# VectorE's instructions of a selective scan interleaved: scans, taps and step sizes between each other, and the next quad's first scan ahead of the high product

## The chip, the cores and the metric

The kernel runs on one core of one Trainium2 chip. The metric is device microseconds from launch to end. Five engines run side by side, each in its own order: TensorE (PE), VectorE (DVE), ScalarE (ACT), GpSimd (POOL) and SyncE (SP, here only a DMA queue). They meet through semaphores alone, also within one engine: an instruction of VectorE that reads what an earlier one of VectorE wrote waits for that one's semaphore.

## The reference, cut

All is float32; two rows of 1024 tokens, 512 wide. The part that takes the time is a state-space layer (1024 inner channels, 16 states each) with a mixture of experts beside it:

```
x, gate = split(xn @ W_in.T);  x = silu(conv4(x))
ts, B, C = rms(split(x @ W_x.T))
dt = softplus(ts @ W_dt.T + b_dt);  A = -exp(A_log)
for t:  state = state * exp(dt_t * A) + (dt_t * x_t) * B_t
        y_t   = sum_n state[n] * C_t[n]
y = (y + x * D) * silu(gate);  s = y @ W_out.T
out = hidden + s * silu(top2_experts(xn))
```

## The kernel before

The 2048 tokens are four chunks of 512 (two chunks a row of the batch); the 1024 channels are eight tiles of 128. Chunk by chunk and tile by tile gives 32 **tiles** n = 0 to 31; chunk c = n // 8, t = n % 8. In chunks 1 and 3 ("odd") the scans start from the state kept by the chunk before. The 16 states of a tile are four **quads** m = 4n to 4n + 3. A quad is four scans r = 0 to 3 of 128 x 512, each holding 32 channels times 4 states on the partitions.

What happens to a quad m:

- POOL writes its drives `drive[m % 4]` (L588, one multiplication of 128 x 2048), and runs up to four quads ahead.
- ACT writes the decays exp(dt * A) into the four PSUM banks `sc` (L801, four instructions). `decays(m, 0)` writes banks 0 and 1, `decays(m, 1)` banks 2 and 3. Since there is only one set of banks, `decays(m + 1, 0)` waits until quad m has left banks 0 and 1, and `decays(m + 1, 1)` until quad m's **high product** has read banks 2 and 3. In even chunks ACT first keeps the two last states (L780).
- DVE runs the four scans (L1175), and multiplies by C (L1185): the **high product** of r = 2, 3 always, the **low product** of r = 0, 1 only in quads that `POOL_QUADS` doesn't give to POOL (then POOL does it, L601, and the two scans write to SBUF, so that their banks come free at once). 94 of 128 low products are POOL's.
- PE sums over the states into `y_ps` (L1426).

Per tile there is more, on every engine in an order written out by hand:

- **Step sizes.** Two tiles ahead PE writes `dt_ps` (L1363), ACT does the softplus (|x|, exp, 1 + e, log: L746 to L758), and DVE ends it in three instructions, each on the one before (L1154, L1156, L1158), and `times_x` (L1150), which multiplies by x. In the tiles that `VECTOR_LOG` leaves out PE adds the parts instead, and DVE has `times_x` alone. ACT copies dt, and a DMA sends both out and back, spread over the partitions, as `rep`.
- **Convolution** of the next chunk, one or two channel tiles per tile for t = 2 to 6 of chunks 0 to 2 (`LATE_X`, `EARLY_X`). ACT copies the projection and applies the first tap (L707, L710); DVE applies the other three (L1114), each on the one before. The late one of a tile is ACT's `copy_x` between `decays(4n + 2, 1)` and `decays(4n + 3, 0)`; on DVE its three taps stand ahead of quad 4n + 3.
- **Gate.** ACT switches its table (1.28 us), does the silu of the gate and of x, and switches back, between `decays(4n + 2, 0)` and `decays(4n + 2, 1)`. DVE's `gate_tile(n - 1)` (L1202) multiplies the summed y by it, after the high product of the first quad of tile n; PE's next sums into `y_ps` wait for that.
- PE also does the gate projection, the experts' slots, the projections of the next chunk and, in the first tiles of a chunk, the output projection of the chunk before.

ACT's order in a tile is: decays(4n, 1), copy dt, decays(4n + 1, 0), copy_x early, decays(4n + 1, 1), decays(4n + 2, 0), tables and silu, decays(4n + 2, 1), copy_x late, decays(4n + 3, 0), decays(4n + 3, 1), softplus(n + 2), decays(4n + 4, 0), with small copies for the experts between. The change leaves it, and the orders of PE, POOL and the DMA queues, alone.

## Time and profile before

| | us |
| --- | --- |
| median of 3 runs | 1072.48 (1071.75 to 1073.99) |
| the profiled execution | 1074.76 |
| its span, first to last instruction | 1072.9 |
| DVE busy | 996.6 (93%) |
| POOL busy | 909.7 (85%) |
| PE busy | 861.6 (80%) |
| ACT busy | 727.6 (68%) |

The profile is one execution. Each view names an instruction by its line, engine, operation and tiles; two of a kind in a row are one line of the timeline ("x2"), with the start of the first and the time to the end of the last. A bracket is idle time of the engine just ahead, and what ended it.

### The profile page before, as it was taken

Reading aid. Unit: us, or ns where it says so; the run is one execution under the profiler, and the core shown is the slowest. Engines: PE = TensorE matmul, PEld = TensorE weight load, DVE = VectorE, ACT = ScalarE, POOL = GpSimd, SP = SyncE. Lnnn points to the kernel's source line nnn. Section 1 sums busy time; section 2 is a strip of 40 time slices with the busy share of each in tenths; the row PEclk is TensorE's granted clock in tenths of the full one; section 3 lists DMA queues with packets and bytes.
Section 4 is the critical chain, followed back from the end, with each engine's and each line's share of the span. In section 5 each row is a group of like instructions: output and inputs, shape, how many; then the busy total and the mean of one; then the engine's idle time right before and its main releaser. Section 6 shows DMA issues by size and latency. Waiting matters only on the chain.

```text
span 1072.9 us, 10234 instructions
## 1 busy us (share of the span) xinstructions
PE 861.6 (80%) x2756; PEld 319.1 (30%) x2756; DVE 996.6 (93%) x1025; ACT 727.6 (68%) x1281; POOL 909.7 (85%) x322
## 2 busy tenths in 40 slices
PE   8943557988978998898846859889897999679568
PEld 5321112333323333333211313333332343223122
DVE  6779988999999989999999899999999989999997
ACT  3657656788787766788565566688777666567543
POOL 0617898997989998888798979799988988999996
PEclk9976668999999999999876879999998999889779
DMA  9847668767778576666743752965648556664725
GB/s 336 345 158 285 223 235 330 278 247 267 263 266 333 183 270 241 228 257 212 259 113 143 217 194 109 320 231 191 228 149 303 217 215 235 216 220 182 274 42 154
DMA packets 86585, 245.93 MB, mean 229 GB/s; under 512 B 9344, under 2 KB 10752, under 8 KB 79872
## 3 DMA queue, kind: packets, MB, share of 16 engines
q1 hardware_dynamic: 67712, 197.03, 51.4%
q10 hardware_dynamic: 12672, 31.46, 7.4%
q0 software_dynamic: 6144, 16.78, 5.8%
q8 instruction: 23, 0.38, 0.1%
q14 instruction: 34, 0.28, 0.1%
HBM read 183.11 MB, written 62.13 MB: 229 GB/s over the span
## 4 chain that ended last, share of the span: by engine, by line
DVE 30%; PE 22%; POOL 21%; issue 11%; DMA 9%; ACT 5%; SPq 2%; DVEq 0%; ACTq 0%; POOLq 0%
DVE sc_ps L1175 13%; POOL drive L588 12%; DVE drive L1175 8%; PE x_ps L1458 5%; POOL drive L601 4%; PE f_ps L1411 4%; DMA rep<-rep_rows 4%; PE y_ps L1426 3%; PE dt_ps L1386 2%; DMA rep_rows<-dtu 2%; DVE x_ps L1114 2%; DVE drive L1185 2%; PE x_ps L1322 2%; POOL moe L573 2%; ACT sc_ps L801 1%
## 5 line engine op out<-in xcount | busy, mean ns | idle before, releaser
L588 POOL TENSOR_TENSOR drive<-rep,b_all 128x2048 f32<-128x2048 f32 x127 | 578.9, 4598 | 46.6 <-DMA rep<-rep_rows 40.5
L801 ACT ACTIVATE sc_ps<-rep,a_neg 128x512 f32<-128x512 f32 x512 | 332.0, 681 | 93.3 <-DVE drive L1185 63.4
L601 POOL TENSOR_TENSOR drive<-drive,c_all 128x1024 f32<-128x1024 f32 x94 | 224.2, 2385 | 20.6 <-ACT state L780 12.8
L1426 PE MATMUL y_ps<-drive,stack 128*32 128x512 f32 x1024 | 153.5, 675 | 107.1 <-POOL drive L601 59.8
L1175 DVE TENSOR_TENSOR_SCAN sc_ps<-sc_ps,state,drive 128x512 f32<-128x512 f32 x164 | 201.0, 1272 | 4.7 <-ACT sc_ps L801 2.4
L1185 DVE TENSOR_TENSOR drive<-sc_ps,c_all 128x1024 f32<-128x1024 f32 x162 | 198.4, 1224 | 5.4
L1175 DVE TENSOR_TENSOR_SCAN sc_ps<-sc_ps,drive 128x512 f32<-128x512 f32 x160 | 186.5, 1211 | 14.6 <-ACT sc_ps L801 7.4
L1411 PE MATMUL f_ps<-w_ring,xT_slot 128*128 128x512 f32 x368 | 171.8, 611 | 14.9 <-ACT xT_slot L811 14.7
L1386 PE MATMUL dt_ps<-xnT,w_g 128*128 128x512 f32 x232 | 126.8, 697 | 27.5 <-ACT dtu L768 27.5
L1175 DVE TENSOR_TENSOR_SCAN drive<-sc_ps,state,drive 128x512 f32<-128x512 f32 x92 | 112.7, 1266 | 3.4 <-ACT sc_ps L801 3.4
L1175 DVE TENSOR_TENSOR_SCAN drive<-sc_ps,drive 128x512 f32<-128x512 f32 x96 | 111.7, 1205 | 0.0
L1411 PEld LDWEIGHTS f_ps<-w_ring,xT_slot 128*128 128x128 f32 x368 | 68.9, 195 | 117.4 <-issue 116.7
L1322 PE MATMUL x_ps<-xnT,w_x 128*128 128x512 f32 x192 | 90.0, 613 | 3.1 <-DMA w_x<-wx_in 3.1
L1458 PE MATMUL x_ps<-w_out,xy 128*128 128x512 f32 x176 | 83.6, 622 | 0.0
L1386 PEld LDWEIGHTS dt_ps<-xnT,w_g 128*128 128x128 f32 x232 | 49.2, 223 | 110.3 <-issue 110.3
L1426 PEld LDWEIGHTS y_ps<-drive,stack 128*32 128x32 f32 x1024 | 21.5, 113 | 199.5 <-issue 119.1
L780 ACT ACTIVATE state<-sc_ps 128x2 f32<-128x2 f32 x80 | 13.4, 168 | 64.5 <-DVE drive L1185 63.1
L1322 PEld LDWEIGHTS x_ps<-xnT,w_x 128*128 128x128 f32 x192 | 35.6, 193 | 56.9 <-issue 52.1
L1420 PE MATMUL y_ps<-xy,diag 128*128 128x512 f32 x64 | 35.5, 638 | 17.8 <-DVE xy L1202 17.8
L1458 PEld LDWEIGHTS x_ps<-w_out,xy 128*128 128x128 f32 x176 | 32.9, 196 | 51.6 <-issue 51.0
L1363 PE MATMUL dt_ps<-dt_in,w_dt 128*128 128x512 f32 x64 | 42.2, 745 | 5.4 <-DVE dt_in L1225 4.2
L811 ACT COPY xT_slot<-f_ps 128x512 f32<-128x512 f32 x46 | 26.6, 578 | 26.1 <-PE f_ps L1400 26.1
(187 smaller groups left out, 1034.0 us busy)
## 6 DMA issues: line engine op xcount, KB each, us to landing
rep<-rep_rows SPq DMA_DIRECT2D x128, 512.0 KB
w_ring<-wring SPq DMA_DIRECT2D x46, 1024.0 KB, 5.4
rep_rows<-dtu ACTq DMA_DIRECT2D x32, 512.0 KB
x_slot<-slot_x SPq DMA_DIRECT2D x46, 256.0 KB, 7.0
slot_rows<-y_slot ACTq DMA_DIRECT2D x46, 256.0 KB
w_g<-wg_in SPq DMA_DIRECT2D x32, 256.0 KB
w_x<-wx_in SPq DMA_DIRECT2D x24, 256.0 KB
slot_x<-zeros SPq DMA_DIRECT2D x1, 5888.0 KB, 20.5
```

The source lines that it names most:

```text
L588: pool.tensor_tensor(drive[:, m % RING, :, :], rep[:, n % 2, :, 1, :], b_all[:, q:q + 1, :].broadcast_to([P, NR, TC]), ALU.mult).then_inc( ...
L601: pool.tensor_tensor(drive[:, m % RING, 0:2, :], drive[:, m % RING, 0:2, :], c_all[:, q:q + 1, :].broadcast_to([P, 2, TC]), ALU.mult).then ...
L801: act.activation(sc[:, r, :], rep[:, n % 2, r, 0, :], ACT.Exp, scale=a_neg[:, lo:lo + 1]).then_inc(decay_ok, 1)
L1175: dve.tensor_tensor_scan(to, sc[:, r, :], drive[:, m % RING, r, :], state[:, lo:lo + 1] if follows else 0.0, ALU.mult, ALU.add).then_inc(s ...
L1185: dve.tensor_tensor(drive[:, m % RING, 2 * h:2 * h + 2, :], sc[:, 2 * h:2 * h + 2, :], c_all[:, q:q + 1, :].broadcast_to([P, 2, TC]), ALU. ...
L1322: last = pe.matmul(x_bank(j), w(h), xnT[:, c % 2, h, :], start=(h == 0), stop=(h == HK - 1))
L1363: pe.matmul(dt_ps[:, :], w_dt[:, t, :], dt_in[:, :], start=True, stop=True).then_inc(dt_mm, 1)
L1386: mm = pe.matmul(gate_bank(c, t)[:, :], w_g[:, h, :], xnT[:, c % 2, h, :], start=(h == 0), stop=(h == HK - 1))
L1411: last = pe.matmul(f_ps[:, :], xT_slot[:, h, :], w_ring[:, j % 2, h, :], start=(h == 0), stop=(h == HK - 1))
L1420: pe.matmul(y_ps[:, :], diag[:, :], xy[:, c % 2, t, :], start=True, stop=False).then_inc(skip_mm, 1)
L1426: last = pe.matmul(y_ps[CH * r:CH * (r + 1), :], stack[:, :], drive[:, m % RING, r, :], start=False, stop=(m % NQ == NQ - 1))
L1458: last = pe.matmul(bank, xy[:, c % 2, t, P * i:P * (i + 1)], w_out[:, t, :], start=(t == 0), stop=(t == NT - 1))
```

## The change

Only VectorE's order changes; it computes the same with as many instructions, and two semaphores more (`tap_sum`, `part_ok`) carry the waits that `link` made.

- The three taps of a convolution stand each between two scans of a quad, no longer in a row.
- The low product stands after scan 2, no longer right after scan 1.
- `scan(m + 1, 0)`, the next quad's first scan, stands ahead of `products(m, 1)` after the second and third quad of each tile. After the first it is the gate that stands ahead of the high product, except in the 13 tiles of `GATE_BEHIND`: there it is again the next quad's scan, and the gate follows the product. After the fourth quad nothing is put between, except in the 12 tiles of `STEPS_AMONG_SCANS`.
- In those 12 tiles the three instructions of the softplus stand around the last scan and the last high product, and `times_x` after the first scan of the next tile.

```diff
+STEPS_AMONG_SCANS = (1, 3, 5, 10, 15, 16, 17, 19, 21, 26, 27, 29)
+GATE_BEHIND = (3, 5, 9, 10, 15, 18, 19, 21, 25, 26, 27, 29, 30)
...
-            def convolve(j):
+            def tap(j, k):
                 c, t = divmod(j, NT)
-                dve.wait_ge(tap_ok, j + 1)
+                if k == 1:
+                    dve.wait_ge(tap_ok, j + 1)
+                else:
+                    dve.wait_ge(tap_sum, 2 * j + k - 1)
...
+            def larger_part(k):
+                dve.wait_ge(ln_ok, k + 1)
...
+            def less_rounding(k):
+                dve.wait_ge(part_ok, 2 * (k - pe_logs(k)) + 1)
...
+            def plus_log(k):
+                dve.wait_ge(part_ok, 2 * (k - pe_logs(k)) + 2)
...
                 if n:
-                    low(m)
+                    scan(m, 0)
+                    if n - 1 in STEPS_AMONG_SCANS:
+                        times_x(n + 1)
+                    scan(m, 1)
                     if pe_log(n + 1):
                         times_x(n + 1)
-                    scans(m, 1)
+                    scan(m, 2)
+                    low_product(m)
+                    scan(m, 3)
                     if chunk_end and not pe_log(n + 1):
                         step_sizes(n + 1)
+                    if n not in GATE_BEHIND:
+                        gate_tile(n - 1)
+                    else:
+                        scan(m + 1, 0)
                     products(m, 1)
-                if n:
-                    gate_tile(n - 1)
-                low(m + 1)
+                    if n in GATE_BEHIND:
+                        gate_tile(n - 1)
+
+                if n not in GATE_BEHIND:
+                    scan(m + 1, 0)
                 if early is not None:
-                    convolve(NT * (c + 1) + early)
-                scans(m + 1, 1)
+                    tap(NT * (c + 1) + early, 1)
+                scan(m + 1, 1)
+                if early is not None:
+                    tap(NT * (c + 1) + early, 2)
+                scan(m + 1, 2)
+                low_product(m + 1)
+                if early is not None:
+                    tap(NT * (c + 1) + early, 3)
+                scan(m + 1, 3)
                 if after_odd and t == 2:
                     out_tile(c - 1, 3)
+                scan(m + 2, 0)
                 products(m + 1, 1)
-                low(m + 2)
+
+                scan(m + 2, 1)
                 if after_odd and t == 1:
                     out_tile(c - 1, 0)
-                high(m + 2)
-                if late is not None:
-                    convolve(NT * (c + 1) + late)
+                scan(m + 2, 2)
+                low_product(m + 2)
+                scan(m + 2, 3)
+                scan(m + 3, 0)
                 if after_odd and t == 1:
                     out_tile(c - 1, 1)
-                low(m + 3)
-                high(m + 3)
-                if rms_tile:
+                products(m + 2, 1)
+
+                if late is not None:
+                    tap(NT * (c + 1) + late, 1)
+                scan(m + 3, 1)
+                if late is not None:
+                    tap(NT * (c + 1) + late, 2)
+                scan(m + 3, 2)
+                low_product(m + 3)
+                if late is not None:
+                    tap(NT * (c + 1) + late, 3)
+                if n in STEPS_AMONG_SCANS:
+                    larger_part(n + 2)
+                scan(m + 3, 3)
+                if n in STEPS_AMONG_SCANS:
+                    less_rounding(n + 2)
+                products(m + 3, 1)
+                if n in STEPS_AMONG_SCANS:
+                    plus_log(n + 2)
+                elif rms_tile:
```

Two places in the program's order on VectorE. The first is tile 4, from its last scans of quad 17 to quad 19 (L1175 is a scan, which the listing calls SCALAR_TENSOR_TENSOR, L1185 a high product, L1114 a tap). Before:

```order
L1175 SCALAR_TENSOR_TENSOR sc_ps<-sc_ps,drive 128x512 x2
L1185 TENSOR_TENSOR drive<-sc_ps,c_all 128x1024
L1175 SCALAR_TENSOR_TENSOR drive<-sc_ps,drive 128x512 x2
L1175 SCALAR_TENSOR_TENSOR sc_ps<-sc_ps,drive 128x512 x2
L1185 TENSOR_TENSOR drive<-sc_ps,c_all 128x1024
L1114 SCALAR_TENSOR_TENSOR x_ps<-x_pad,cw,x_ps 128x512 x2
L1114 SCALAR_TENSOR_TENSOR xy<-x_pad,cw,x_ps 128x512
L1175 SCALAR_TENSOR_TENSOR drive<-sc_ps,drive 128x512 x2
L1175 SCALAR_TENSOR_TENSOR sc_ps<-sc_ps,drive 128x512 x2
L1185 TENSOR_TENSOR drive<-sc_ps,c_all 128x1024
```

The same piece on VectorE in the change, from quad 18's first scan, which stands right behind quad 17's last (scans are L1190, high products L1200, taps L1119 there):

```order
L1190 SCALAR_TENSOR_TENSOR drive<-sc_ps,drive 128x512
L1200 TENSOR_TENSOR drive<-sc_ps,c_all 128x1024
L1190 SCALAR_TENSOR_TENSOR drive<-sc_ps,drive 128x512
L1190 SCALAR_TENSOR_TENSOR sc_ps<-sc_ps,drive 128x512 x2
L1190 SCALAR_TENSOR_TENSOR drive<-sc_ps,drive 128x512
L1200 TENSOR_TENSOR drive<-sc_ps,c_all 128x1024
L1119 SCALAR_TENSOR_TENSOR x_ps<-x_pad,cw,x_ps 128x512
L1190 SCALAR_TENSOR_TENSOR drive<-sc_ps,drive 128x512
L1119 SCALAR_TENSOR_TENSOR x_ps<-x_pad,cw,x_ps 128x512
L1190 SCALAR_TENSOR_TENSOR sc_ps<-sc_ps,drive 128x512
L1119 SCALAR_TENSOR_TENSOR xy<-x_pad,cw,x_ps 128x512
L1190 SCALAR_TENSOR_TENSOR sc_ps<-sc_ps,drive 128x512
```

The first scan of quad 18 and that of quad 19 have moved ahead of the high products of quads 17 and 18, and the first scan of quad 19 now also stands ahead of all three late taps.

The second place is the end of tile 3 and the start of tile 4 on VectorE, a tile of `STEPS_AMONG_SCANS` (L1154, L1156, L1158 and L1150 are the step sizes). Before:

```order
L1175 SCALAR_TENSOR_TENSOR sc_ps<-sc_ps,drive 128x512 x2
L1185 TENSOR_TENSOR drive<-sc_ps,c_all 128x1024
L1154 SCALAR_TENSOR_TENSOR dt_ps<-dt_ps,t_e 128x512
L1156 SCALAR_TENSOR_TENSOR dt_ps<-t_w,dt_ps 128x512
L1158 TENSOR_TENSOR dt_ps<-t_l,dt_ps 128x512
L1150 TENSOR_TENSOR dtu<-dt_ps,xy 128x512
```

In the change (L1159, L1164, L1169 and L1155):

```order
L1159 SCALAR_TENSOR_TENSOR dt_ps<-dt_ps,t_e 128x512
L1190 SCALAR_TENSOR_TENSOR sc_ps<-sc_ps,drive 128x512
L1164 SCALAR_TENSOR_TENSOR dt_ps<-t_w,dt_ps 128x512
L1200 TENSOR_TENSOR drive<-sc_ps,c_all 128x1024
L1169 TENSOR_TENSOR dt_ps<-t_l,dt_ps 128x512
L1190 SCALAR_TENSOR_TENSOR drive<-sc_ps,drive 128x512
L1155 TENSOR_TENSOR dtu<-dt_ps,xy 128x512
```

The first of the softplus's three now stands ahead of the last scan, and `times_x` behind the next tile's first.

## Rows read from the trace of the kernel before

**Rows 1.** The page's head, and its busy time of each engine.
```profile
span 1072.9 us, 10234 instructions
PE 861.6 (80%) x2756; PEld 319.1 (30%) x2756; DVE 996.6 (93%) x1025; ACT 727.6 (68%) x1281; POOL 909.7 (85%) x322
```
**Rows 2.** Busy time by stretch: length, PE, PEld, DVE, ACT, POOL, clock, DMA, GB/s.
```profile
568.00:612.70 44.70, 31.39 (x95) 10.90 (x95) 41.41 (x40) 25.19 (x45) 42.53 (x22) 0.81 0.52 155
906.60:1030.40 123.80, 92.71 (x306) 32.59 (x299) 118.11 (x107) 79.46 (x125) 121.39 (x41) 0.86 0.62 213
```
**Rows 3.** Waits of VectorE, whole span: us in total, times, longest.
```profile
DVE dt_ps L1154 <- ACT t_l L755: 10.2, 7, 3.7
DVE sc_ps L1175 <- ACT sc_ps L801: 9.8, 8, 2.7
```
**Rows 4.** Timeline of VectorE in tile 4: start, us, instruction.
```profile
217.50 2.33 DVE L1175 TENSOR_TENSOR_SCAN drive<-sc_ps,drive 128x512 f32<-128x512 f32 x2
219.75 1.52 DVE L1114 SCALAR_TENSOR_TENSOR x_ps<-x_pad,cw,x_ps 128x512 f32<-128x512 f32 x2
...
221.97 2.34 DVE L1175 TENSOR_TENSOR_SCAN sc_ps<-sc_ps,drive 128x512 f32<-128x512 f32 x2
224.35 1.22 DVE L1185 TENSOR_TENSOR drive<-sc_ps,c_all 128x1024 f32<-128x1024 f32 x1
...
231.23 1.54 DVE L1114 SCALAR_TENSOR_TENSOR x_ps<-x_pad,cw,x_ps 128x512 f32<-128x512 f32 x2
...
233.47 2.33 DVE L1175 TENSOR_TENSOR_SCAN drive<-sc_ps,drive 128x512 f32<-128x512 f32 x2
```
**Rows 5.** Timeline of ScalarE in tile 4, from quad 18's first decays.
```profile
219.87 0.20 ACT L780 ACTIVATE state<-drive 128x2 f32<-128x2 f32 x1 [0.82 <-DVE drive L1175]
...
221.42 1.28 ACT L941 ACT_TABLE_LOAD   x1
...
224.37 1.28 ACT L949 ACT_TABLE_LOAD   x1
...
229.39 1.30 ACT L801 ACTIVATE sc_ps<-rep,a_neg 128x512 f32<-128x512 f32 x2
```
**Rows 6.** Timeline of VectorE in tile 10.
```profile
390.92 1.23 DVE L1185 TENSOR_TENSOR drive<-sc_ps,c_all 128x1024 f32<-128x1024 f32 x1
393.13 0.69 DVE L1202 TENSOR_TENSOR xy<-y_ps,gate 128x512 f32<-128x512 f32 x1 [0.99 <-PE y_ps L1426]
394.77 2.46 DVE L1175 TENSOR_TENSOR_SCAN drive<-sc_ps,state,drive 128x512 f32<-128x512 f32 x2 [0.94 <-ACT sc_ps L801]
...
407.73 1.55 DVE L1114 SCALAR_TENSOR_TENSOR x_ps<-x_pad,cw,x_ps 128x512 f32<-128x512 f32 x2 [0.90 <-ACT x_ps L710]
```
**Rows 7.** Timeline of VectorE from tile 23 into tile 24.
```profile
817.81 1.22 DVE L1185 TENSOR_TENSOR drive<-sc_ps,c_all 128x1024 f32<-128x1024 f32 x1
...
825.31 2.46 DVE L1175 TENSOR_TENSOR_SCAN drive<-sc_ps,state,drive 128x512 f32<-128x512 f32 x2 [0.54 <-ACT sc_ps L801]
```
**Rows 8.** Timeline of ScalarE from tile 23 into tile 24.
```profile
819.27 1.30 ACT L801 ACTIVATE sc_ps<-rep,a_neg 128x512 f32<-128x512 f32 x2
821.03 0.60 ACT L746 ACTIVATE t_e<-dt_ps 128x512 f32<-128x512 f32 x1 [0.46 <-PE dt_ps L1363]
...
824.49 1.30 ACT L801 ACTIVATE sc_ps<-rep,a_neg 128x512 f32<-128x512 f32 x2
```
**Rows 9.** Timeline of tile 17, VectorE and ScalarE.
```profile
622.71 1.22 DVE L1185 TENSOR_TENSOR drive<-sc_ps,c_all 128x1024 f32<-128x1024 f32 x1
...
630.69 1.30 ACT L801 ACTIVATE sc_ps<-rep,a_neg 128x512 f32<-128x512 f32 x2
...
631.47 2.34 DVE L1175 TENSOR_TENSOR_SCAN sc_ps<-sc_ps,drive 128x512 f32<-128x512 f32 x2
```
**Rows 10.** Timeline of VectorE where it waits for POOL.
```profile
612.70 2.35 DVE L1175 TENSOR_TENSOR_SCAN sc_ps<-sc_ps,drive 128x512 f32<-128x512 f32 x2 [1.98 <-POOL drive L588]
...
1030.45 2.47 DVE L1175 TENSOR_TENSOR_SCAN sc_ps<-sc_ps,state,drive 128x512 f32<-128x512 f32 x2 [2.35 <-POOL drive L588]
```

More of the change, by code:

```diff
@@ L1103, in route_weights, with convolve @@
                 dve.tensor_tensor(p2[:, :], e2, r1, ALU.mult).then_inc(prob_ok, 1)
-            def convolve(j):
+            def tap(j, k):
                 c, t = divmod(j, NT)
-                dve.wait_ge(tap_ok, j + 1)
-                if c == 1:
+                if k == 1:
+                    dve.wait_ge(tap_ok, j + 1)
+                else:
+                    dve.wait_ge(tap_sum, 2 * j + k - 1)
+                if k == K - 1 and c == 1:
                     dve.wait_ge(s_stage, 16 * (NCH - 2))
                     dve.wait_ge(lgT_mm, 1)
-                if c >= 2:
+                if k == K - 1 and c >= 2:
                     dve.wait_ge(o_mm, TT * (c - 1))
+                dve.scalar_tensor_tensor(out=x_bank(j) if k < K - 1 else xy[:, c % 2, t, :], in0=padded(j)[:, k:k + TC],
+                                         scalar=cw[:, t * K + k:t * K + k + 1], in1=x_bank(j),
+                                         op0=ALU.mult, op1=ALU.add).then_inc(tap_sum if k < K - 1 else conv_ok, 1)
+            def convolve(j):
                 for k in range(1, K):
-                    tap = dve.scalar_tensor_tensor(out=x_bank(j) if k < K - 1 else xy[:, c % 2, t, :], in0=padded(j)[:, k:k + TC],
-                                                   scalar=cw[:, t * K + k:t * K + k + 1], in1=x_bank(j),
-                                                   op0=ALU.mult, op1=ALU.add)
-                    if k < K - 1:
-                        link(tap)
-                    else:
-                        tap.then_inc(conv_ok, 1)
+                    tap(j, k)
             spreads(1)
@@ L1169, in scans @@
                 if follows:
-                    dve.wait_ge(state_ok, kept_states(m - NQ * NT) + h + 1)
-                for r in (2 * h, 2 * h + 1):
-                    lo = column(t, q, r)
-                    to = drive[:, m % RING, r, :] if h == 0 and on_pool(m) else sc[:, r, :]
-                    dve.wait_ge(decay_ok, NR * m + r + 1)
-                    dve.tensor_tensor_scan(to, sc[:, r, :], drive[:, m % RING, r, :],
-                                           state[:, lo:lo + 1] if follows else 0.0,
-                                           ALU.mult, ALU.add).then_inc(scan_ok, 1)
+                    dve.wait_ge(state_ok, kept_states(m - NQ * NT) + r // 2 + 1)
+                lo = column(t, q, r)
+                to = drive[:, m % RING, r, :] if r < 2 and on_pool(m) else sc[:, r, :]
+                dve.wait_ge(decay_ok, NR * m + r + 1)
+                dve.tensor_tensor_scan(to, sc[:, r, :], drive[:, m % RING, r, :],
+                                       state[:, lo:lo + 1] if follows else 0.0,
+                                       ALU.mult, ALU.add).then_inc(scan_ok, 1)
             def products(m, h):
@@ L1187, in products, with low_product @@
                                   ALU.mult).then_inc(high_ok if h else low_ok, 1)
-            def low(m):
-                scans(m, 0)
+            def low_product(m):
                 if not on_pool(m):
                     products(m, 0)
-            def high(m):
-                scans(m, 1)
-                products(m, 1)
             def gate_tile(n):
@@ L1232, in _ @@
             route_rows()
-            for h in range(2):
-                scans(0, h)
-                products(0, h)
+            scan(0, 0)
+            scan(0, 1)
+            low_product(0)
+            scan(0, 2)
+            scan(0, 3)
+            products(0, 1)
             route_weights()
@@ L1245, in _ @@
                 if n:
-                    low(m)
+                    scan(m, 0)
+                    if n - 1 in STEPS_AMONG_SCANS:
+                        times_x(n + 1)
+                    scan(m, 1)
                     if pe_log(n + 1):
                         times_x(n + 1)
-                    scans(m, 1)
+                    scan(m, 2)
+                    low_product(m)
+                    scan(m, 3)
                     if chunk_end and not pe_log(n + 1):
                         step_sizes(n + 1)
+                    if n not in GATE_BEHIND:
+                        gate_tile(n - 1)
+                    else:
+                        scan(m + 1, 0)
```

21 lines of the change are left out of this document (12 added, 9 removed).

## The prediction

> **What bounds the kernel now.** Read the busy times first [rows 1]: VectorE is busy 996.6 of 1072.9 us and POOL 909.7, so VectorE is the first suspect and POOL the second. Then the busy times by stretch [rows 2] and where VectorE waits for POOL [rows 10]. In two stretches POOL hardly stops (42.53 of 44.70 us, and 121.39 of 123.80), and at the end of each VectorE stands waiting for a drive (1.98 and 2.35 us). In those 169 us it is POOL that sets the pace; work that VectorE saves there buys nothing, and up to about 2 us that it loses costs nothing. In the rest VectorE is nearly always busy. Its waits are short and mostly for ScalarE [rows 3]: 10.2 us for the logarithm and 9.8 us for decays. That looks like one engine that is the bound. The timelines of one tile [rows 4, 5] say more: VectorE and ScalarE pass the four banks back and forth, and ScalarE has stretches without idle time that end just ahead of the scan that needs them. So the question isn't only how much VectorE's work shrinks, but whether ScalarE's next decay is there earlier.
>
> **What goes.** An instruction of VectorE that doesn't wait for the one ahead starts before that one's profiled end: the scans at 217.50 end at 219.83, the first tap starts at 219.75, 0.08 us earlier [rows 4]. One that waits for the result of the one ahead starts after it: the scans at 221.97 end at 224.31, the high product starts at 224.35, 0.04 us later. The difference is 0.12 us a pair. Pairs that the change takes apart, counted in the program: 103 high products (124 stood right behind their scan; 20 at a tile's end and one before the loop stay), 33 low ones, 48 taps (24 convolutions, two each), 36 in the 12 tiles of step sizes: 220. 220 x 0.12 = 26 us of VectorE's time. No DMA and no wait on another engine is removed.
>
> The row shows 0.12 us for each wait of this kind. The Trainium skill speaks against that (VectorE: DVE Perf Modes, section "The DRAIN you can't avoid"): eight copies take as long with a semaphore after each as with one after the last, "the semaphore costs nothing extra here". By that rule the saving would be 0 and not 26 us; the trace disagrees with it, by the 0.12 us between the two kinds of pair.
>
> **What the moved steps cost.** Steps of VectorE, from start to next start [rows 4]: a scan 1.12 us (2.25 for two), a high product 1.22 - 0.08 = 1.14, a tap behind something else 0.67, three taps in a row 2.22.
>
> *Tile 4, the late convolution.* ScalarE's chain starts when quad 17's second scan ends, at 219.83, and is without idle time from 219.87: keep states, quad 18's decays, table, silu, table, decays of banks 2 and 3, a copy, copy_x (late), and quad 19's first decay at 229.39 [rows 5], done half of 1.30 us later, at 230.04: 10.2 us after the scan. Before, VectorE needed quad 19's first scan only at 233.47, 13.6 us after it: 3.4 us of cover. In the new order what stands between is two taps, two scans, quad 18's first scan, one high product and three scans: 1.33 + 2.24 + 1.12 + 1.14 + 3.36 - 0.08 = 9.1 us. The high product and the late taps, 1.14 + 2.24, have gone behind quad 19's first scan and cover nothing. VectorE waits 10.2 - 9.1 = 1.1 us. The tile saves 7 pairs, 0.84. Net +0.3 us. This is because the taps stand where ScalarE has its copy_x, and the scan has been moved past them. Worked in the same way, tiles 3, 5, 20 and 21 give 0 to +0.3 each (the first decay of their last quad also waits for PE's projection), and 11 to 13, where no states are kept, -0.1 each. Together +0.8.
>
> *Tiles 7 and 23, the softplus at the end.* With the next scan ahead of it, the third quad's high product, at 817.81, ends about one scan later (1.12 and a short wait, less two pairs: +1.0). It frees the banks for ScalarE's last decays at 819.27, and behind them in ScalarE's order stand the softplus (821.03, where it had 0.46 us to wait for PE) and the next tile's decays at 824.49, for which VectorE already waits 0.54 us at 825.31 [rows 7, 8]. So most of it is passed on: +0.8, and in tile 7 about +0.9: +1.7.
>
> *Tile 17, low products on VectorE.* ScalarE's chain starts here with the low product, which ends at 623.93; the second decay pair of quad 70 begins at 630.69 and its first is done at 631.34, 7.4 us later, and VectorE needs it at 631.47 [rows 9]. There is no cover at all. Now the low product comes a scan later (+1.12), and the next quad's low product (1.14) has moved from ahead of that scan to behind it. Against it stand 11 pairs, 1.3 us, and a wait for the first step size instruction that now comes about 2.4 us sooner. I take +1.4. Tiles 1 and 14 have the same form: +1.2 and +0.4. Tiles 16 and 30 lie in POOL's stretches. Tile 31 is the last: +0.7.
>
> *Tile 10, the gate behind.* The first high product, at 390.92, is done at 392.15, in the shadow of two waits, for the gate's sums (0.99) and for decays (0.94) [rows 6]. Moved behind the scan that ends this wait at 394.77, it and the gate cost 1.14 + 0.60 us there. 0.90 is given back at 407.73, where VectorE waits for copy_x anyway; but quad 43's first scan now stands ahead of quad 42's high product, and copy_x ahead of that scan's decay. +1.0, between 0 and +2.4. Tiles 25 and 26 have the same form; there it is PE, busy without a break, that sets when the next rep is sent, and only the later gate counts: +0.7. In tile 19 the moved scan fills a wait for the gate, but two later ones appear at quads 78 and 79, about a scan each, against its 11 pairs: I take +1.3, from below nothing to 2; its neighbour 18 +0.2.
>
> *Step sizes among the scans.* The first of them needs the logarithm, which ends 3.7 us after the high product of the third quad, since that frees ScalarE's last decays (1.30 us) and four activations follow. In tiles 26, 27 and 29 VectorE is there after two scans: 1.4 us of wait against 0.84 saved. They lie in POOL's second stretch, whose cover is 2.35 us; I count +0.5. Tiles 6 and 22 (one convolution, the rms) come to +0.35 each; 8, 15 and 24 save 0.3 each, since they have no late tap.
>
> **Sum.** 0.8 + 1.7 + 1.4 + 1.2 + 0.4 + 0.7 + 1.0 + 0.7 + 1.3 + 0.2 + 0.5 + 0.7 - 0.9 = +9.7 us. Each of these is worked on the clock of its own tile; existing waits behind them will take some, as the one at 612.70 [rows 10] for what tiles 14 and 1 lose ahead of it, and I take off 2. The profiled execution is 1074.76 us, 2.3 above the median, so 1074.76 + 7.7 = 1082.5, and against the median 1080. What measures as different from no change is about 0.2%, 2 us.
>
> **Rivals.** (1) *ScalarE gives way.* VectorE is 93% busy and ScalarE 68% [rows 1], so it may be that waits of a microsecond in a tile are caught up by the next one, where ScalarE has slack, and the 26 us arrive outside POOL's two stretches: 26 x (1 - 169/935) = 21, 935 us being the loop behind 137 us. Less the few hard waits (5) the time is 1072.5 - 16 = 1056. For it speaks that VectorE's waits are only some 20 us in all; against it the chain of rows 5, which is as long as the tile gives room for. (2) *Half of it.* The stalls come out at half of what I worked out, as when ScalarE's copies come earlier with their inputs: 26 us is saved, of which a third stays over: -8, 1064. The decider is whether quad 4n + 3's first scan waits in the late tiles; from a wait under 0.8 us on the tile gains. (3) *Even*, within 2 us of 1072.5. (4) *Worse.* The later high products delay PE's sums and with them POOL's ring, and every tile of `STEPS_AMONG_SCANS` waits 1.4 us for its logarithm: 12 x 1.4 = 17 less what is counted: 1092. (5) *No pair costs anything*, so that only the moved waits are left. VectorE comes later by the 0.12 us of each pair, which makes its waits shorter: +12, 1084. Rows 4 speak against it; the Trainium skill, in the section named above, would have it so.
>
> **Chances.** Forecast (1074.6 to 1088) 0.46; worse 0.07; no pair costs anything 0.02; even 0.13; half 0.20; ScalarE gives way 0.12. That makes slower 0.55, the same 0.13, faster 0.32. The forecast's own range is 1075 to 1088. The range reaches down to the half gain and to the upper part of ScalarE's giving way, to 1058, and up to 1091.
>
> **What the new profile would show.** Right: high products start 0.08 us ahead of the end of what stands before them, and VectorE's busy time hardly falls while its waits for ScalarE's decays grow from 9.8 to 30 us or more, most of them at the first scan of a tile's last quad (tiles 3 to 5, 10 to 13, 18 to 21); in tiles 26, 27 and 29 a wait for the logarithm; at the start of tiles 8 and 24 a wait for decays of 1 us. Wrong: tile 4 shorter than before, those waits absent. The forecast is wrong in the main if ScalarE's decays for the last quad come earlier than 10.2 us after the scan that starts their chain.

## The result, and the profile after

The change makes the kernel slower: 1085.47 us (median of 4 runs, 1083.90 to 1088.65) against 1072.12, a ratio of 1.0125 (95% interval 1.0107 to 1.0143). The predicted time was 1080.0, from 1058 to 1091.

The page of the kernel after, its head and the busy time of each engine:

```profile
span 1084.2 us, 10364 instructions
PE 859.8 (79%) x2756; PEld 319.6 (29%) x2756; DVE 976.2 (90%) x1025; ACT 728.0 (67%) x1281; POOL 910.2 (84%) x322
```

Against [rows 1] the span is 11.3 us longer, VectorE's busy time 20.4 us shorter, and the others are as they were. So VectorE has its saving, and 31.7 us more of idle time. The waits of VectorE after (us in total, times, longest) say for whom:

```profile
DVE drive L1190 <- ACT sc_ps L804: 28.6, 15, 5.1
DVE sc_ps L1190 <- ACT sc_ps L804: 20.2, 18, 2.6
DVE dt_ps L1159 <- ACT t_l L758: 15.6, 13, 3.7
DVE sc_ps L1190 <- POOL drive L591: 7.7, 4, 4.9
DVE xy L1212 <- PE y_ps L1477: 2.4, 1, 2.4
```

The two upper rows are scans that wait for decays: 48.8 us. Before, the row of [rows 3] has 9.8, and its sister (scans that write `drive`) has 3.4. Two more rows of the kernel before:

```profile
DVE xy L1202 <- PE y_ps L1426: 7.1, 5, 2.1
DVE drive L1175 <- ACT sc_ps L801: 3.4, 4, 0.9
```

So decays cost 35.6 us more, and the logarithm (15.6 against 10.2) 5.4 more. The other way went the gate's wait for PE, from 7.1 to 2.4, and the gaps inside the dependent pairs: some 0.03 us in each of the 220, 7 us.

Tile 4 after, on VectorE (start, us, instruction, and idle time in brackets):

```profile
219.35 1.21 DVE L1190 TENSOR_TENSOR_SCAN drive<-sc_ps,drive 128x512 f32<-128x512 f32 x1
...
227.39 2.32 DVE L1190 TENSOR_TENSOR_SCAN sc_ps<-sc_ps,drive 128x512 f32<-128x512 f32 x2
230.91 1.22 DVE L1190 TENSOR_TENSOR_SCAN drive<-sc_ps,drive 128x512 f32<-128x512 f32 x1 [1.20 <-ACT sc_ps L804]
232.05 1.20 DVE L1200 TENSOR_TENSOR drive<-sc_ps,c_all 128x1024 f32<-128x1024 f32 x1
233.16 0.74 DVE L1119 SCALAR_TENSOR_TENSOR x_ps<-x_pad,cw,x_ps 128x512 f32<-128x512 f32 x1
```

and on ScalarE:

```profile
220.59 0.20 ACT L783 ACTIVATE state<-drive 128x2 f32<-128x2 f32 x1 [0.77 <-DVE drive L1190]
...
229.08 0.78 ACT L713 ACTIVATE x_ps<-x_pad,cb,cw 128x512 f32<-128x512 f32 x1
...
230.11 1.30 ACT L804 ACTIVATE sc_ps<-rep,a_neg 128x512 f32<-128x512 f32 x2
```

The scan at 219.35 ends at 220.56 and starts ScalarE's chain; the first of quad 19's two decays is done at 230.11 + 0.65 = 230.76. That is 10.2 us, as forecast, and the wait is 1.20 us where 1.1 was forecast. Behind the waiting scan stand the high product and the tap that could have filled it.

### The profile page after: what moved, and what is told of

The parts are those of the page before. It is cut to its first block, busy times and chain, and to the rows that moved or that the text cites. A ratio compares the mean times of both kernels' runs of the same rounds, so it can differ in the third digit from the quotient of the medians.

```text
span 1084.2 us, 10364 instructions
## 1 busy us (share of the span) xinstructions
PE 859.8 (79%) x2756; PEld 319.6 (29%) x2756; DVE 976.2 (90%) x1025; ACT 728.0 (67%) x1281; POOL 910.2 (84%) x322
## 4 chain that ended last, share of the span: by engine, by line
DVE 24%; PE 24%; issue 15%; POOL 14%; ACT 13%; DMA 7%; SPq 2%; ACTq 1%; DVEq 0%; POOLq 0%
POOL drive L591 8%; DVE sc_ps L1190 8%; DVE drive L1200 6%; PE x_ps L1509 5%; ACT sc_ps L804 5%; PE f_ps L1462 5%; DVE drive L1190 4%; PE x_ps L1373 4%; POOL drive L604 3%; DMA rep<-rep_rows 2%; PE y_ps L1477 2%; DMA w_x<-wx_in 2%; DMA rep_rows<-dtu 2%; PE dt_ps L1437 2%; PE x_ps L1395 1%
## 5 line engine op out<-in xcount | busy, mean ns | idle before, releaser
L1190 DVE TENSOR_TENSOR_SCAN sc_ps<-sc_ps,state,drive 128x512 f32<-128x512 f32 x164 | 203.0, 1271 | 11.9 <-ACT sc_ps L804 11.3
L1190 DVE TENSOR_TENSOR_SCAN sc_ps<-sc_ps,drive 128x512 f32<-128x512 f32 x160 | 189.6, 1214 | 16.9 <-ACT sc_ps L804 8.9
L1200 DVE TENSOR_TENSOR drive<-sc_ps,c_all 128x1024 f32<-128x1024 f32 x162 | 195.3, 1206 | 0.8
L1437 PE MATMUL dt_ps<-xnT,w_g 128*128 128x512 f32 x232 | 123.7, 682 | 23.9 <-ACT dtu L771 23.7
L1190 DVE TENSOR_TENSOR_SCAN drive<-sc_ps,state,drive 128x512 f32<-128x512 f32 x92 | 115.6, 1268 | 15.9 <-ACT sc_ps L804 15.6
L1190 DVE TENSOR_TENSOR_SCAN drive<-sc_ps,drive 128x512 f32<-128x512 f32 x96 | 115.2, 1208 | 13.8 <-ACT sc_ps L804 13.0
L626 POOL TENSOR_SCALAR rep<-rep,moe 128x512 f32<-128x512 f32 x8 | 16.5, 2065 | 30.7 <-DVEq L1137 30.7
L1119 DVE SCALAR_TENSOR_TENSOR x_ps<-x_pad,cw,x_ps 128x512 f32<-128x512 f32 x54 | 39.7, 736 | 2.0 <-ACT x_ps L713 1.8
```

Source lines behind the costliest of these rows:

```text
L1119: dve.scalar_tensor_tensor(out=x_bank(j) if k < K - 1 else xy[:, c % 2, t, :], in0=padded(j)[:, k:k + TC], scalar=cw[:, t * K + k:t * K + ...
L1190: dve.tensor_tensor_scan(to, sc[:, r, :], drive[:, m % RING, r, :], state[:, lo:lo + 1] if follows else 0.0, ALU.mult, ALU.add).then_inc(s ...
L1200: dve.tensor_tensor(drive[:, m % RING, 2 * h:2 * h + 2, :], sc[:, 2 * h:2 * h + 2, :], c_all[:, q:q + 1, :].broadcast_to([P, 2, TC]), ALU. ...
L1437: mm = pe.matmul(gate_bank(c, t)[:, :], w_g[:, h, :], xnT[:, c % 2, h, :], start=(h == 0), stop=(h == HK - 1))
```

## The change, tile by tile

A tile is taken from the start of its quad 4n's second scan to that of the next tile. Its length after less its length before, in the two profiled executions, beside the prediction's terms (us):

| tiles | forecast | measured |
| --- | --- | --- |
| 3, 4, 5, 11, 12, 13, 20, 21 (late) | +0.8 | +3.0 |
| 7, 23 | +1.7 | +2.4 |
| 17 | +1.4 | +3.3 |
| 1, 14 | +1.6 | +1.1 |
| 31 | +0.7 | +2.0 |
| 10 | +1.0 | +2.2 |
| 25, 26 | +0.7 | +4.8 |
| 18, 19 | +1.5 | -1.3 |
| 27, 28, 29 | +0.5 | -0.3 |
| 6, 22 | +0.7 | -0.8 |
| 8, 15, 24 | -0.9 | -0.6 |
| 0, 2, 9, 16, 30 (forecast: what existing waits take back, in no tile in particular) | -2.0 | -4.5 |
| sum | +7.7 | +11.3 |

Each column of lengths is one execution, and two things in the differences aren't the order's. The profiled execution of before has a wait in tile 27, here on VectorE:

```profile
934.30 2.47 DVE L1175 TENSOR_TENSOR_SCAN sc_ps<-sc_ps,state,drive 128x512 f32<-128x512 f32 x2 [2.04 <-ACT sc_ps L801]
```

The kernels c1, d1 and d2 below leave tile 26 as long as before and don't have it; their tile 27 is 1.75 to 2.2 us shorter than before's, as the change's is (-1.8). And the execution after has two long DMA issues on ScalarE, in tiles 12 and 26 (last section): tile 12 is 1.6 us longer than its like, 11 and 13, and tile 26 is 1.2 us longer than in a3, a4 and d3. A difference of a tile says something where several kernels agree on it.

## The experiments

All but three (a4, e1 and the version chosen by tile, which also move ScalarE's copy_x) change the order of VectorE alone. The ratio is to the kernel before on the same chip.

| kernel | median | ratio (95% interval) |
| --- | --- | --- |
| the change | 1085.47 | 1.0125 (1.0107 to 1.0143) |
| a1 scans ahead alone | 1087.55 | 1.0143 (1.0121 to 1.0165) |
| a2 the change without them | 1071.38 | 0.9993 (0.9980 to 1.0006) |
| a3 product and late tap first | 1073.04 | 1.0006 (0.9993 to 1.0019) |
| a4 decay ahead of copy_x | 1072.78 | 1.0010 (0.9992 to 1.0028) |
| e1 a4's edit on the kernel before | 1073.45 | 1.0012 (0.9999 to 1.0024) |
| c4 no scan ahead of the gate in 10, 25, 26 | 1081.68 | 1.0091 (1.0073 to 1.0110) |
| c1 low product later, alone | 1078.29 | 1.0065 (1.0045 to 1.0084) |
| d3 the change, low product back | 1083.76 | 1.0119 (1.0096 to 1.0142) |
| c2 step sizes among scans, alone | 1068.66 | 0.9969 (0.9954 to 0.9984) |
| d1 taps apart, alone | 1070.80 | 0.9991 (0.9976 to 1.0005) |
| d2 gate ahead, alone | 1072.64 | 1.0006 (0.9991 to 1.0021) |
| c3 parts chosen by tile | 1061.95 | 0.9903 (0.9886 to 0.9920) |

**The scans ahead, alone and left out.** a1 adds them to the order of before, a2 takes them out of the change.

```diff
 (a1, on before)                        (a2, on the change)
                 scan(m + 1, 3)                         scan(m + 1, 3)
+                scan(m + 2, 0)         -               scan(m + 2, 0)
                 products(m + 1, 1)                     products(m + 1, 1)
-                scan(m + 2, 0)         +               scan(m + 2, 0)
```

> The order of before, with one part of the change: the next quad's first scan ahead of the high product, in the same 77 places (31 or 32 each after the second and third quad, 13 after the first). Taps in a row, low products, gate and step sizes stay as before. Theory (ScalarE's chain sets the pace, and the moved scans and products lose their cover): in a late tile two taps fewer stand between the scan that starts ScalarE's chain and quad 4n + 3's first scan, so the cover is 2.24 + 1.12 + 1.14 + 3.36 = 7.9 us against a chain of 10.2: a wait of 2.3 us in 12 tiles, 28 us, plus about 9 us of the gate put behind in tiles 10, 25 and 26 and of the ends of tiles 7 and 23, less 77 x 0.12 = 9 us saved: 1085 to 1100, slower than the whole change. Rival (interleaving taps, low products and step sizes is what costs, moved scans gain): 9 us less than before, outside POOL's stretches: 1064 to 1068.

> The change without its scans ahead of high products: taps, low products, step sizes and the gate stay interleaved as in the change (in the 13 tiles with the gate behind, the product comes first and the gate right after it, as before). Theory: the waits at the first scan of the last quad (18.3 us in 12 late tiles by the profile after), those in tiles 10, 25 and 26 (12.9 us against 2.8 before) and about 2 us in tiles 7 and 23 go nearly all, 77 pairs of 0.12 us come back: 1085.5 - 18 - 10 - 2 + 9 = 1065, and 1063 to 1072 since some waits will move on. Rival (the interleaving costs it): 1080 or more.

The totals lie in the theory's ranges: a1 is 15.1 us above its before, a2 is 1.1 below. The moved scans alone cost as much as the whole change, and without them nothing is lost. But a2 isn't at the 1065 that was worked out: its other 143 pairs, 17 us of VectorE's time, bring hardly anything, since waits rise here too. In the waits of a2 the scans' waits for decays are 23.6 us, against 48.8 in the change and 13.2 before:

```profile
DVE sc_ps L1195 <- ACT sc_ps L809: 17.3, 17, 2.7
DVE drive L1195 <- ACT sc_ps L809: 6.3, 7, 1.8
```

One step of a1's expectation is wrong: a wait of 2.3 us in each late tile. The twelve waits come to 15.4 us, not 28, and tile 4's is 1.18. VectorE there in a1:

```profile
226.08 1.20 DVE L1205 TENSOR_TENSOR drive<-sc_ps,c_all 128x1024 f32<-128x1024 f32 x1
...
231.83 1.22 DVE L1195 TENSOR_TENSOR_SCAN drive<-sc_ps,drive 128x512 f32<-128x512 f32 x1 [1.18 <-ACT sc_ps L809]
```

and ScalarE:

```profile
227.31 0.17 ACT L788 ACTIVATE state<-sc_ps 128x2 f32<-128x2 f32 x1 [0.91 <-DVE drive L1205]
```

With the early taps in a row, ScalarE's chain doesn't run through from quad 17's second scan. It stops for 0.91 us at quad 17's high product, which now comes a scan late, and starts there a second time. From that product to quad 19's first scan VectorE has three scans, 3.4 us, for 4.4 us of ScalarE's work. The wait is that of the later release. In the change itself both releases come at nearly the same time.

**What makes the moved scan wait.** a3 gives VectorE its cover back in the late tiles, a4 shortens ScalarE's chain and leaves VectorE alone.

```diff
 (a3, VectorE, late tiles)
-                scan(m + 3, 0)
                 products(m + 2, 1)
                 tap(NT * (c + 1) + late, 1)
+                scan(m + 3, 0)
+                tap(NT * (c + 1) + late, 2)
                 scan(m + 3, 1)
 (a4, ScalarE)
-                if late is not None:
-                    copy_x(NT * (c + 1) + late)
                 store_slot(b, first_slot)
                 decays(m + 3, 0)
+                if late is not None:
+                    copy_x(NT * (c + 1) + late)
```

> The whole change, but in the 12 tiles with a late convolution the high product of quad 4n + 2 and the first late tap stand ahead of quad 4n + 3's first scan (the taps stay apart: tap, scan, tap, scan, tap, scan). Theory: this puts 1.14 + 0.65 us of cover back, more than the 1.2 us wait of tile 4; of 18.3 us of waits at these scans some 4 stay, 12 to 14 us are gained: 1071 to 1075. Rival (the wait is only passed on, since ScalarE or the tables are the bound of these tiles in any order): within 3 us of 1085.

> VectorE's order exactly as in the change; on ScalarE alone the late copy_x (its four activations, 1.8 us in tile 4) is moved from ahead of decays(4n + 3, 0) to behind it. Theory: the decay is there 1.8 us earlier, the waits of quad 4n + 3's first scan fall from 18.3 us in the 12 tiles to about 3, and the taps, which need copy_x, stand a scan and a product (2.26 us) behind that scan and hardly wait: 1070 to 1076. Rival (it is not copy_x; the wait is that for banks or drives): 1083 to 1088.

Both give 12 to 13 us back and end even with the kernel before. The twelve waits, 18.3 us in the change, are 0.3 us in a3 and 0.7 in a4. Tile 4 in a3, on VectorE, has no wait at the scan at 228.92:

```profile
227.12 1.23 DVE L1205 TENSOR_TENSOR drive<-sc_ps,c_all 128x1024 f32<-128x1024 f32 x1
228.26 0.75 DVE L1124 SCALAR_TENSOR_TENSOR x_ps<-x_pad,cw,x_ps 128x512 f32<-128x512 f32 x1
228.92 1.22 DVE L1195 TENSOR_TENSOR_SCAN drive<-sc_ps,drive 128x512 f32<-128x512 f32 x1
```

In a4 ScalarE makes the decays at 226.44 and copies behind them:

```profile
226.44 1.30 ACT L810 ACTIVATE sc_ps<-rep,a_neg 128x512 f32<-128x512 f32 x2
227.68 0.19 ACT L714 ACTIVATE x_pad<-halo 128x3 f32<-128x3 f32 x1
```

so that VectorE goes on at 227.24 with the scan. The first tap of copy_x (the activation at 228.43, 0.78 us long) is done at 229.21, and VectorE's tap comes at 229.49 without a wait. It might be that a4's edit is a gain of its own, so it was also put on the kernel before:

> VectorE's order of before, with ScalarE's edit alone: in the late tiles decays(4n + 3, 0) ahead of copy_x. Theory: before, the decay has 3.4 us of cover in tile 4 and nobody waits for it, so an earlier one buys nothing, and the three taps, which stand ahead of that scan there, get their first tap 1.5 us later, with 3.4 - 2.2 = 1.2 us or so to spare: waits for copy_x appear in some of the 12 tiles, 0 to +6: 1071 to 1077. Rival (the edit is a gain of its own, whatever VectorE's order, and the run of the whole change with it says nothing of the moved scans): -5 to -13, 1059 to 1067.

It isn't: +0.8 us, within or just above no change. At the scans in question VectorE doesn't wait in the kernel before, nor in e1. Its waits in e1 show the price of the earlier decay, the taps' waits for copy_x, 4.8 us against 2.0 before:

```profile
DVE x_ps L1127 <- ACT x_ps L719: 4.8, 5, 1.1
```

Of these two orders of VectorE, the edit pays only in the one that needs that decay early.

e1 settles one more thing. The change has 130 instructions more than the kernel before (10364 against 10234), all of them semaphore waits of VectorE. Every kernel of the table has them, e1 too, with VectorE's order of before; so they are not what makes the change slower.

**The gate in tiles 10, 25 and 26.** The timeline of VectorE in tile 10 after, where [rows 6] has product, gate and scan with waits of 0.99 and 0.94 us:

```profile
391.14 2.44 DVE L1190 TENSOR_TENSOR_SCAN sc_ps<-sc_ps,state,drive 128x512 f32<-128x512 f32 x2
397.47 1.28 DVE L1190 TENSOR_TENSOR_SCAN drive<-sc_ps,state,drive 128x512 f32<-128x512 f32 x1 [3.89 <-ACT sc_ps L804]
...
412.49 1.29 DVE L1190 TENSOR_TENSOR_SCAN sc_ps<-sc_ps,state,drive 128x512 f32<-128x512 f32 x1 [2.65 <-ACT sc_ps L804]
```

VectorE stands 3.89 us with a high product and a gate queued behind. c4 puts the scan back in these three tiles:

```diff
-                    scan(m + 1, 0)
                     products(m, 1)
                     gate_tile(n - 1)
+                    scan(m + 1, 0)
```

> The whole change, but in tiles 10, 25 and 26 quad 4n + 1's first scan doesn't stand ahead of the first high product: product, gate, scan, as before. Theory: the wait of 3.9, 3.9 and 5.1 us in one piece before that scan falls back to two of 0.99 and 0.94, and the 1.14 + 0.6 us of product and gate lie in its shadow again: 1.9 us in each of the three, of which tile 27 gives back 1.8: -4, 1080 to 1083. Rival (these stretches are PE's or POOL's in any order): 1085 to 1086.

The ratio falls from 1.0125 to 1.0091, 3.6 us, as the theory has it. In the profile tile 10 goes from +2.2 to +1.0, tile 25 from +1.25 to 0.0 and tile 26 from +3.55 to +0.6. Of this last step 1.2 us are the change's long DMA issue, which c4 doesn't have there.

**The low product.** In tile 17 after, on VectorE:

```profile
634.07 0.69 DVE L1218 TENSOR_TENSOR moe<-x_ps,moe 128x512 f32<-128x512 f32 x1 [0.83 <-ACT moe L882]
...
636.21 1.23 DVE L1190 TENSOR_TENSOR_SCAN sc_ps<-sc_ps,drive 128x512 f32<-128x512 f32 x1 [1.45 <-ACT sc_ps L804]
```

and on ScalarE:

```profile
628.76 0.17 ACT L783 ACTIVATE state<-sc_ps 128x2 f32<-128x2 f32 x1 [2.98 <-DVE drive L1200]
...
635.49 1.30 ACT L804 ACTIVATE sc_ps<-rep,a_neg 128x512 f32<-128x512 f32 x2
```

ScalarE idles 2.98 us for the later low product, and from its end at 628.73 to the first decay at 636.14 it works 7.4 us without a break, as in [rows 9]. Two things wait for it, the multiplication of the output rows and the scan. The moved step alone, and the change without it:

```diff
 (c1, on before)                        (d3, on the change)
                 scan(m, 1)                             scan(m, 1)
-                low_product(m)         +               low_product(m)
                 scan(m, 2)                             scan(m, 2)
+                low_product(m)         -               low_product(m)
```

> The order of before with one part of the change: the low product of VectorE's 33 quads one scan later (the one ahead of the loop stays), nothing else. Theory (where VectorE makes the low product, ScalarE's chain starts with it): tiles 17, 31, 1, 14 lose about what they lose in the run without scans ahead, 2.5, 2.1, 0.75 and 0.3, and 30 up to 0.8, and the others save about 1 us: +4 to +5, 1075 to 1078. The prediction's terms for these tiles come to +3.7. Rival (the pair is all that matters): 33 x 0.12 = 4 less, 1068.5.

> The whole change, but each low product right behind scan 1, as before. Theory: what the low product costs alone (6 us by the medians) comes back here too, mostly in tiles 17, 31, 14 and 1: -4 to -7 against the change, 1078 to 1082. Rival (the waits of moved scans swallow it, since they end on the same chain of ScalarE): -2 to +1, 1083 to 1086.

Alone it costs 6 us by the medians, a little more than the 4 to 5 expected, and 3.6 by its profiled execution (5.6 without the wait in tile 27 of before), +2.0 in tile 17, +2.3 in 31 and +1.4 in 14. In the whole change its removal can't be told from nothing (1.0119 against 1.0125): the 4 to 7 us of the expectation didn't come back, and the time lies in the rival's range. The profile of d3 shows both halves: tile 17 is +1.2 where the change has +3.3, and tile 31 +0.65 where it has +2.0. But tiles 15 and 16, around the wait for POOL's drive of [rows 10], are +0.3 and +0.7 where the change has -0.3 and -0.95. The two costs overlap; that this is since both wait for the same chain of ScalarE, as the rival has it, is argued and not shown for each tile. How much of the change's time is the low product's stays open, between 0 and 3 us or so.

**The parts that save.**

```diff
 (c2, on before)                        (d1, on before)
+    larger_part(n + 2)                 -    convolve(NT * (c + 1) + late)
     scan(m + 3, 3)                          scan(m + 3, 0)
+    less_rounding(n + 2)               +    tap(NT * (c + 1) + late, 1)
     products(m + 3, 1)                      scan(m + 3, 1)
+    plus_log(n + 2)                    +    tap(NT * (c + 1) + late, 2)
-    step_sizes(n + 2)                       scan(m + 3, 2)
     scan(m + 4, 0)                     +    tap(NT * (c + 1) + late, 3)
+    times_x(n + 2)                          scan(m + 3, 3)
```

> The order of before with one part of the change: the step sizes among the scans in the 12 tiles. Theory: 36 pairs of 0.12 are 4.3 us, of which 1.1 lie in tiles 26, 27 and 29, where VectorE comes for the logarithm 1.4 us too early, and some more in tiles 15 and 16, ahead of POOL's hard wait: -2 to 0, 1070 to 1072.5. Rival (the prediction's worse case, a wait of 1.4 us for the logarithm in each of the 12): +6 to +12, 1078 to 1084.

> The order of before with one part of the change: the taps of the 24 convolutions apart, each between two scans; the late ones stand behind quad 4n + 3's first scan. No scan ahead of a product. Theory: tile 4 has 3.4 us of cover ahead of that scan before, the three taps are 2.2 of it, so 1.2 stay and no wait comes: all 48 pairs are saved, 5.8 us, less what tile 16's wait for POOL and tile 10's for copy_x take: -4 to -6, 1066 to 1068. Rival (already this takes the cover, and the decay comes late): a wait of some 0.5 us or more in the late tiles, 1070 to 1076.

c2 saves 3.6 us by the medians of the 4.3 that 36 pairs are worth, more than expected. d1 was expected to save 4 to 6 and saves 0.5 by the medians, which can't be told from nothing. Its tiles say why: 4, 11, 12, 13 and 20 are 0.53 us shorter each, four pairs at 0.13. But tile 5 is 1.0 longer, tile 19 1.0 and tile 10 0.5. At the first scan of the last quad, where no late tile waited before, VectorE now waits 0.55, 0.76 and 1.71 us in these three, and 0.87 and 0.39 in tiles 2 and 21. The rest of tiles 5 and 19 is something else: in tile 5 a wait of 0.77 us for the early copy_x, behind a DMA issue of 1.78 us, and in tile 19 a wait for the gate's sums of 2.53 us where it was 2.11. VectorE in tile 10 of d1:

```profile
408.31 1.29 DVE L1195 TENSOR_TENSOR_SCAN sc_ps<-sc_ps,state,drive 128x512 f32<-128x512 f32 x1 [1.71 <-POOL drive L596]
```

The drive that is named is done at 408.22, and ScalarE's decay, made at 407.51, at 408.15. So both came at the same time, 1.7 us after VectorE. With the taps ahead, [rows 6] has 0.90 at copy_x, and no wait at the scan. The expectation had taken tile 4's 3.4 us of cover for every late tile.

The third part, the gate ahead of the product in 18 tiles:

```diff
                     scan(m, 3)
+                    gate_tile(n - 1)
                     products(m, 1)
-                    gate_tile(n - 1)
```

> The order of before with one part of the change: the gate ahead of the first high product in the 18 tiles outside the list. Theory: 18 pairs of 0.12 us against a high product that comes 0.6 us later for ScalarE: -2 to +1, 1070 to 1073.5; in the profile no wait that wasn't there. Rival (PE's sums aren't done in time and the product queues behind the gate's wait): +3 to +8.

No change that can be told from nothing (+1.4 us by the medians, within noise). The profile isn't free of new waits, as was expected: VectorE waits 1.38 us for copy_x in tile 4 and 2.00 us for a decay in tile 6, where it didn't wait before.

By the medians the parts alone come to +15.1, +6.0, -3.6, -0.5 and +1.4, 18.4 us, against 13.4 for the whole. So they don't add; that they share waits is seen in d3 for the low product and the moved scans.

**A version that beats both.** The idea is that a step is moved only where its cover stays. Which tiles these are was read off the traces of before, the change and a1 to a4, tile by tile; the runs with one part alone had no share in it.

```diff
-    scans ahead everywhere, low products later everywhere
+    late tiles 2, 4, 5, 18 to 21: a3's order
+    late tiles 3, 10 to 13: the change's order, with a4's on ScalarE
+    tiles 10, 25, 26: no scan ahead of product and gate
+    tiles 7, 23: no scan ahead of the third quad's product
+    tiles 1, 16, 17, 31: no scan ahead, gate behind
+    low product later: 7 to 13, 18, 24
+    step sizes among scans: 3, 5, 10, 15, 19, 21
+    tiles 6, 22: taps in a row
```

> The parts of the change chosen by tile. Late tiles 2, 4, 5 and 18 to 21: product and first tap ahead of quad 4n + 3's first scan. Tiles 3 and 10 to 13: the change's order on VectorE, and on ScalarE decays(4n + 3, 0) ahead of the late copy_x. Tiles 10, 25, 26: no scan ahead of product and gate. Tiles 7 and 23: none ahead of the third quad's product. Tiles 1, 16, 17, 31: no scans ahead, gate behind. Low products a scan later only in tiles 7 to 13, 18 and 24; step sizes among scans only in 3, 5, 10, 15, 19, 21; taps in a row in tiles 6 and 22. Theory: waits stay where they were before and each tile saves its pairs: tile by tile from the four traces so far -0.7 to -1.1 in the late ones (12 tiles), 1.2 in 22, some 0.5 in 8, 9 and 23: 11 to 14 us in all, 1057 to 1063. Rival (POOL is nearly the bound: it is busy 910 us, and what VectorE saves outside its two stretches turns up as waits for drives): 1067 to 1072.

1061.95 us, 1.0% faster than before (0.9886 to 0.9920) and 2.2% faster than the change. Its page and its waits:

```profile
PE 858.5 (81%) x2756; PEld 317.2 (30%) x2756; DVE 983.0 (93%) x1025; ACT 727.3 (69%) x1281; POOL 909.6 (86%) x322
```

```profile
DVE sc_ps L1198 <- ACT sc_ps L810: 10.5, 12, 1.9
DVE drive L1198 <- ACT sc_ps L810: 8.7, 10, 2.2
DVE sc_ps L1198 <- POOL drive L597: 8.0, 3, 3.8
```

VectorE's busy time falls by 13.6 us and the median by 10.4. The waits for decays rise by 6 us only (19.2 against 13.2), and those for POOL don't grow (8.0 against 9.4), so POOL hasn't become the bound. No run takes this version apart, so what each of its choices is worth isn't shown.

## Why the prediction was right, and where its sizes were off

**The bound and the place: right.** The new waits are for ScalarE's decays, 35.6 us more of them, and about half of this stands at the first scan of a late tile's last quad: 12 waits, 18.3 us. In tile 4 the chain of 10.2 us, the cover of 9.1 and the wait of 1.1 came out within 0.1 us. a3 and a4 show the cause from both sides, a2 that the moved scans are the part that costs, and e1 that before, nobody waited for that decay.

**What a pair is worth: right.** 220 pairs at 0.12 us are 26 us. Busy time fell by 20.4, and another 7 us or so were the gaps inside the pairs. In the trace of before 336 instructions of VectorE start 0.01 to 0.07 us behind the end of the one ahead, in the change 117. In d1 four pairs less made a tile 0.53 us shorter. What the Trainium skill says of eight copies (VectorE: DVE Perf Modes, section "The DRAIN you can't avoid"), that a semaphore after each costs nothing extra, doesn't carry over to this kernel's pairs of scans, taps and products, in which one waits for what the one ahead wrote: 0.12 to 0.13 us each. "VectorE's busy time hardly falls" was wrong, and against the prediction's own rows: two instructions that overlap by 0.08 us are busy 0.08 us less together.

**Late tiles: too low, +0.8 against +3.0, or +1.4 without a long DMA issue.** Tile 4 is right (+0.3); tiles 5 (+0.9), 21 (+0.95) and 12 (+1.15) are not. ScalarE in tile 5 after:

```profile
249.96 0.20 ACT L783 ACTIVATE state<-drive 128x2 f32<-128x2 f32 x1
...
258.54 0.59 ACT L710 COPY x_pad<-x_ps 128x512 f32<-128x512 f32 x1 [0.67 <-PE x_ps L1373]
...
260.26 1.30 ACT L804 ACTIVATE sc_ps<-rep,a_neg 128x512 f32<-128x512 f32 x2
```

Here the chain takes 11.0 us from the scan's end at 249.93, since copy_x also waits 0.67 us for PE's projection, and VectorE waits 1.98 us. I had named that wait for the projection, and not put it into the sum. Tile 21 has the same wait of 1.98. Tile 12 isn't the order's: ScalarE stood 1.99 us behind a DMA issue there (last section), VectorE then waited 0.70 us for the early copy_x and 1.13 at the last quad, and in d3, without that, the tile is -0.3.

**The gate behind: right in kind, +1.7 against +7.0 in tiles 10, 25 and 26.** For 25 and 26 the step that failed is "it is PE that sets when the next rep is sent, and only the later gate counts". c4 shows that the scan ahead of product and gate is the whole cost there: tile 25 loses all its 1.25 us when the scan is put back. Of tile 26's +3.55, 1.2 us are the long DMA issue. The 1.8 us less in tile 27 aren't given back by the order, since c1, d1 and d2 have them too. In tile 10 the 0.90 that was to be given back at copy_x came as a wait of 2.65 for the decay instead.

**Low products: near in tiles 1 and 14 (+1.6 against +1.1), less than half of it in 17 and 31 (2.1 against 5.2).** In tile 17 I had counted the wait of the scan, and not that of the output rows' multiplication, which waits for the same stretch of ScalarE (0.83 us). A later one of 1.81 us for PE's sums of the next output rows isn't the low product's, since d3 has 1.73 of it; its cause stays open. In tile 31 the wait is the scan's alone, 2.47 us, and 2.32 in c1; the prediction has no working for its +0.7.

**Tile 19: the wrong sign, +1.3 against -2.0.** The moved scan filled the wait for the gate (2.11 us before), as forecast; but of the two waits of about a scan each that I put at quads 78 and 79 only one came, 1.62 us, and the 11 pairs were saved.

**Ends of tiles 7 and 23: +1.7 against +2.4.** The wait at the start of tile 24, 0.54 us in [rows 7], has become, on VectorE:

```profile
832.21 2.46 DVE L1190 TENSOR_TENSOR_SCAN drive<-sc_ps,state,drive 128x512 f32<-128x512 f32 x2 [1.11 <-ACT sc_ps L804]
```

**Step sizes: the wait is right.** In tiles 26, 27 and 29 VectorE comes for the logarithm 1.35 us too early, where 1.4 was forecast; tile 27 after:

```profile
951.93 0.70 DVE L1159 SCALAR_TENSOR_TENSOR dt_ps<-dt_ps,t_e 128x512 f32<-128x512 f32 x1 [1.35 <-ACT t_l L758]
```

In tiles 3, 5, 10, 15, 19 and 21 there is no such wait, and 0.56 us in 1, 16 and 17, so the worse case (1.4 us in each of the 12 tiles) did not come. The term's total (+0.5 against -0.3) says little, since tile 27 is in it.

Put together, the sign and the mechanism were right, and the forecast of 1080.0 is 5.5 us below the measured median. In the two profiled executions the sum is 3.6 us short (7.7 against 11.3). The four terms of late tiles, gate behind, low products and tile 19 are short by 6.8 us together, and the others give 3.2 back; the two long DMA issues, 2.8 us in all, and the 2.0 us in tile 27 of before are in these figures too. So that the total came so near is partly luck, and the range from 1058 to 1091 is so wide that three of the five rivals' times (1064, 1084 and no change) lie in it as well.

## What to carry to other kernels

Before an instruction is moved to hide a fixed cost, ask what its old place covered: here a high product and three taps, 3.4 us of work, stood where VectorE would otherwise have waited for ScalarE, and 26 us saved between instructions were paid for with waits for decays of 48.8 us instead of 13.2. Work out for each engine that is passed a buffer back and forth how long its chain is from its release to the next use, and compare that with the work that stands between on the waiting engine, in both orders and for both releases of the buffer. Such a reordering is a decision place by place: applied everywhere, the parts added 1.25% to the time; chosen tile by tile, with two other orders in the late tiles, one of them with ScalarE's decay ahead of its copies, they took 1.0% off it.

## What the runs showed of the hardware that was not expected

Issuing a DMA on ScalarE's queue can hold ScalarE for long, and not always equally long. Rows of the kernel after, of ScalarE in tiles 10, 12 and 26:

```profile
395.80 0.80 ACTq L845 DMA_DIRECT2D s_rows<-zeros  x1
...
459.00 2.21 ACTq L830 DMA_DIRECT2D slot_rows<-y_slot  x1
461.26 1.30 ACT L804 ACTIVATE sc_ps<-rep,a_neg 128x512 f32<-128x512 f32 x2 [1.99 <-issue]
...
902.89 2.01 ACTq L845 DMA_DIRECT2D s_rows<-zeros  x1
904.94 1.30 ACT L804 ACTIVATE sc_ps<-rep,a_neg 128x512 f32<-128x512 f32 x2 [2.16 <-issue]
```

In all three the decays stand behind the issue. A run has eight issues of `s_rows`. In the 14 profiles of this study 110 of the 112 took 0.33 us or 0.79 to 0.80, always the same time at the same place, and two of them, both in tile 26, 2.01 and 2.10 us (the latter in the version chosen by tile). Of the 644 issues of `slot_rows` three in four took 0.33 us, and 17, in ten of the kernels and in changing tiles, 1.02 to 2.39 us. The one in tile 26 makes the wait there 5.10 us where tiles 10 and 25 have 3.89 and 3.88. Why an issue takes longer now and then isn't shown. It does mean that the profiles of two executions can differ by a microsecond or two in a tile for no reason of the order.
